# A two-layer conditioned attention kernel: reordering and rebuilding the work of its first 65 microseconds

## The chip, the cores and the metric

The kernel runs on one core of a Trainium2 chip. The metric is device time in microseconds (us), lower is better. A core has five engines with instruction queues of their own: PE (TensorE, matrix products into PSUM), ACT (ScalarE), DVE (VectorE), POOL (GpSimd) and SP (SyncE, which here issues all DMAs). They wait for each other through semaphores only.

## The reference, cut to what matters

32 batches of 256 tokens with 256 features pass through two attention layers. Layer 0 is softmax attention with 16 heads of 16 features, layer 1 is linear attention. Each ends in a modulation whose scale and shift come from an embedding `cond` of 512 numbers per batch.

```python
# layer 0, x: (32, 256, 256), emb: (32, 512)
xn = layer_norm(x) * norm_w + norm_b
q = (xn @ q_w + q_b).reshape(B, T, 16, 16);  k, v likewise
att = einsum('bnhl,bmhl->bnmh', q, k) + (1.0 - mask) * -1000000.0
y = einsum('bnmh,bmhl->bnhl', softmax(att, axis=2), v)      # over the keys
e = silu(emb) @ emb_w + emb_b                               # (32, 512) @ (512, 512)
scale, shift = split(e)
h = layer_norm(y) * sb_norm_w + sb_norm_b
x = x + silu(h * (1 + scale) + shift) @ out_w + out_b
# layer 1: q softmaxed over a head's 16 features, k softmaxed over the tokens, then
# y = q @ (k^T v) per head; the same modulation, with weights film_emb_W of its own
```

The rows that a layer norm's bias adds to a product (`norm_b @ q_w` and the like) are worked out once, at the start, and added to the projections' biases.

## The kernel before

One program keeps the work of all batches in a pipeline that is written out by hand: a turn `t` is one batch's step, with eight slots `i` in a turn, and each engine walks through `for t: for i: slot(t, i)` in that fixed order. Batch `t` enters in turn `t`:

- slot 0: PE turns the normed rows (`xturn`); slot 1: ACT copies the result rounded (`xturned`, `xT`), DVE makes its low part (`xlow`);
- slots 2, 4, 6: PE multiplies by the query, key and value weights (`qk(t, 0)`, `qk(t, 1)`, `vals`), each as three products of high and low parts; ACT adds the bias (`qk`), POOL splits the sum in a high and a low part (`split`, semaphores `s_hi`, then `s_lo`), and SP copies the parts of 16 heads into the layout of the scores (`parts`, tiles `Qs`, `Ks`; key rows 7 of 32 get the mask from DRAM, `mask_parts`);
- from 13 slots later on (`LAG_M`): PE makes scores for the row maximum (`rowmax`, eight per batch, tile `psM`) and DVE reduces them (`reduce`, tile `cm`). `psM` is there once, so each `rowmax` waits for the reduce of the one before;
- from 26 slots later on (`LAG_S`): the scores again, their exponentials (ACT) and the product with the values (`values`), four heads side by side in column tiles of the array;
- layer 1 follows in rounds of its own (`second`), after the last turn of layer 0.

What happens once stands between these slots. In turn 0 PE makes `column` (query bias, key bias) and `row` (value bias, from which DVE makes `vbx`, which the last matmul of `vals` adds). From slot (1, 5) to (2, 4) PE makes the embeddings' product, a piece `embed(c)` in each slot: 128 columns of the weights `EW` are the stationary side, and the 32 columns of `cT` (the activated embeddings, turned) stream. In (2, 1) to (2, 6) stand the bias columns and rows of layer 1. Some names in the rows: L1033 is a product of parts, L1052 `column`, L1059 `row`, L1065 `embed`, L1088 the scores, L1103 `rowmax`, L1124 `values`, L1155 `xturn`, L801 the reduce of a `rowmax`, L381 and L384 the split's high and low part, L263 and L266 the copies of `parts`.

Of the kernel before, what the change touches and what calls it, by code (L numbers as in the profile page):

```python
# [51 lines left out]
def bass_cond_seq_kernel(nc, x, cond, mask_f, mask_i, weights, emb, cols, rows, ident_d, diag_d, fill, out):  # L52
# [4 lines left out]
    with ExitStack() as ctx:  # L57
# [128 lines left out]
        p_fill, p_vb, s_cond = sem("p_fill"), sem("p_vb"), sem("s_cond")  # L186
        s_md = sem("s_md")
# [28 lines left out]
        def _(sp):  # L216
# [39 lines left out]
            def parts(n, w):  # L256

                sp.wait_ge(s_lo, 2 * n + w + 1)
                if n >= RING:
                    sp.wait_ge(s_sT, 8 * (n - RING) + 8)  # L260
                dst, b = (Qs, Ks)[w][n % RING], s_in[w][n % RING]
                for r, part in enumerate(((0, 1, 0), (0, 0, 1))[w]):
                    sp.dma_start(dst[r:128:4, :, :], qp[w][:, part, :, :]).then_inc(b, 16)  # L263
                if w:
                    for o in range(2):
                        sp.dma_start(dst[64 * o + 7:64 * o + 64:32, :, :],  # L266
                                     md[n].rearrange("c (a t) -> c a t", a=1).to_broadcast([2, 8, T])).then_inc(b, 16)
# [227 lines left out]
        def _(a):  # L495
# [164 lines left out]
            def slot(t, i):  # L660
# [53 lines left out]
        def _(v):  # L714
# [56 lines left out]
            def film(step):  # L771
                if step == 0:
                    v.wait_ge(p_act, 6)
# [190 lines left out]
            def slot(t, i):  # L964
# [8 lines left out]
                if (t, i) == (1, 4):  # L973
                    v.wait_ge(p_act, 4)
# [5 lines left out]
                if (t, i) == (2, 7):  # L980
                    v.wait_ge(p_pe, 7)
                    v.tensor_tensor(rb[:, 2, :], rb[:, 2, :], psT[1][:, 0:256], ALU.add)
                    v.tensor_tensor(rb[:, 3, :], rb[:, 3, :], psT[1][:, 512:768], ALU.add).then_inc(p_ve, 1)
# [42 lines left out]
        def _(pe):  # L1026
# [293 lines left out]
            def slot(t, i):  # L1320
                if (t, i) == (0, 1):
                    pe.wait_ge(s_ld[1], 16 * LOADS[1])
                if t == 0 and i in (1, 3):
                    pe.wait_ge(s_lw[i // 2], 16)
                    column(psM[i // 2][:, 0:2], 0, i // 2).then_inc(p_pe, 1)
                if (t, i) == (0, 3):
# [13 lines left out]
                if (t, i) == (1, 5):  # L1340
                    pe.wait_ge(p_act, 4)
                    pe.wait_ge(p_film, 2)
                    pe.wait_ge(s_ld[2], 16 * LOADS[2])
                if (t, i) == (3, 2):
                    pe.wait_ge(p_act, 6)
# [19 lines left out]
                if (t, i) == (2, 3):  # L1365
                    column(psT[0][:, 514:516], 1, 2)
                if (t, i) == (2, 5):
                    row(psT[1][:, 0:256], 1, 0)
                if (t, i) == (2, 6):
                    row(psT[1][:, 512:768], 1, 2).then_inc(p_pe, 1)  # L1370
# [83 lines left out]
```

## Time and profile before

| | us |
|---|---|
| three runs | 988.84, 990.59, 982.50 (median 988.84) |
| the profiled execution | 986.95 |
| its span, first to last instruction | 985.2 |

| engine | busy us | share of the span |
|---|---|---|
| PE | 929.1 | 94% |
| DVE | 771.3 | 78% |
| ACT | 708.9 | 72% |
| POOL | 584.9 | 59% |

Busy time is that of the recorded instructions. PE's clock has two levels, 2.4 GHz (granted clock 1.00) and half of it (0.50); the profile gives the mean of a stretch. Between 140 and 540 us it is 1.00. The chain that ended last is followed back from the last instruction, each piece with its start and its length.

### The profile page before, as it was taken

Reading aid. Unit: us, or ns where it says so; the run is one execution under the profiler, and the core shown is the slowest. Engines: PE = TensorE matmul, PEld = TensorE weight load, DVE = VectorE, ACT = ScalarE, POOL = GpSimd, SP = SyncE. Lnnn points to the kernel's source line nnn. Section 1 sums busy time; section 2 is a strip of 40 time slices with the busy share of each in tenths; the row PEclk is TensorE's granted clock in tenths of the full one; section 3 lists DMA queues with packets and bytes.
Section 4 is the critical chain, followed back from the end, with each engine's and each line's share of the span. In section 5 each row is a group of like instructions: output and inputs, shape, how many; then the busy total and the mean of one; then the engine's idle time right before and its main releaser. Section 6 shows DMA issues by size and latency. Waiting matters only on the chain.

```text
span 985.2 us, 24979 instructions
## 1 busy us (share of the span) xinstructions
PE 929.1 (94%) x8916; PEld 774.2 (79%) x8916; DVE 771.3 (78%) x1536; ACT 708.9 (72%) x1326; POOL 584.9 (59%) x1033
## 2 busy tenths in 40 slices
PE   5989999999999999999999757999999999999996
PEld 5867676777777777777777435999999999999995
DVE  5357998888888888888887734788888888888874
ACT  2137677777777777777777665688888888888874
POOL 3234364646464646464646134688888888888874
PEclk9689999999999999999999988999999999999998
DMA  6733333343434343333333222112222322223111
GB/s 223 244 100 136 114 135 136 118 153 117 154 126 146 112 158 133 138 134 137 135 126 122 93 71 71 60 65 76 77 76 89 99 79 76 77 77 92 56 28 54
DMA packets 77403, 108.63 MB, mean 110 GB/s; under 512 B 7072, under 2 KB 43392, under 8 KB 77152
## 3 DMA queue, kind: packets, MB, share of 16 engines
q1 hardware_dynamic: 77280, 107.03, 32.2%
q8 instruction: 72, 1.18, 0.5%
q14 instruction: 51, 0.42, 0.1%
HBM read 35.60 MB, written 16.88 MB: 53 GB/s over the span
## 4 chain that ended last, share of the span: by engine, by line
PE 82%; DVE 7%; issue 6%; POOL 2%; ACT 1%; DMA 1%; SPq 1%; POOLq 0%; DVEq 0%; ACTq 0%
PE psX L1033 14%; PE psY L1124 12%; PE psT L1033 10%; PE psM L1033 9%; PE psM L1103 8%; PE psT L1088 7%; PE psY L1033 4%; PE psT L1272 3%; PE psT L1044 3%; PE psM L1044 3%; PE psY L1241 3%; DVE sb_cm L801 3%; PE psY L1143 2%; DVE sb_yr L818 2%; PE psX L1044 1%
## 5 line engine op out<-in xcount | busy, mean ns | idle before, releaser
L801 DVE TENSOR_REDUCE sb_cm<-psM 128x4 f32<-128x1024 f32 x256 | 313.5, 1224 | 98.1 <-PE psM L1103 89.3
L511 ACT ACTIVATE sb_P<-psT 128x1024 f32<-128x1024 f32 x256 | 262.1, 1025 | 16.9 <-PE psT L1088 13.7
L1124 PE MATMUL psY<-sb_P,sb_Vp 128*17 128x256 f32 x2048 | 137.9, 387 | 8.8 <-DVE sb_yr L818 8.3
L367 POOL TENSOR_SCALAR sb_ve<-sb_mv 128x2 f32<-128x2 f32 x32 | 7.1, 222 | 230.3 <-DVE sb_mv L826 230.3
L1103 PE MATMUL psM<-sb_Ks,sb_Qs 64*128 64x256 f32 x1024 | 119.9, 312 | 12.2 <-DVE sb_cm L801 10.7
L1088 PEld LDWEIGHTS psT<-sb_Qs,sb_Ks 64*128 64x128 f32 x1024 | 78.2, 188 | 60.2 <-issue 54.0
L1088 PE MATMUL psT<-sb_Qs,sb_Ks 64*128 64x256 f32 x1024 | 119.8, 313 | 0.0
L525 ACT ACTIVATE sb_qp<-psX,sb_bq 128x256 f32<-128x256 f32 x122 | 51.2, 471 | 79.8 <-PE psX L1033 77.7
L1103 PEld LDWEIGHTS psM<-sb_Ks,sb_Qs 64*128 64x128 f32 x1024 | 78.4, 188 | 31.9 <-DVE sb_cm L801 14.9
L1033 PE MATMUL psX<-sb_xT,sb_W0h 128*128 128x256 f32 x488 | 96.0, 300 | 0.8
L1124 PEld LDWEIGHTS psY<-sb_P,sb_Vp 128*17 128x17 f32 x2048 | 49.4, 97 | 53.2 <-issue 15.6
L384 POOL TENSOR_TENSOR sb_qp<-sb_qp 128x512 fp32r<-128x512 f32 x64 | 82.5, 1290 | 5.3
L1033 PEld LDWEIGHTS psX<-sb_xT,sb_W0h 128*128 128x128 f32 x488 | 73.2, 196 | 6.5 <-DVE sb_xT L808 6.3
L381 POOL TENSOR_SCALAR sb_qp<-sb_qp 128x512 fp32r<-128x512 f32 x64 | 39.8, 622 | 49.5 <-ACT sb_qp L525 47.6
L549 ACT ACTIVATE sb_yT<-psY 128x256 f32<-128x256 f32 x128 | 49.3, 385 | 23.9 <-PE psY L1124 23.9
L418 POOL TENSOR_TENSOR sb_rs<-sb_ve,sb_ph 128x2 f32<-128x2 f32 x64 | 54.6, 854 | 5.3
L1033 PE MATMUL psT<-sb_W1l,sb_xT 128*128 128x256 f32 x256 | 51.6, 283 | 0.0
L1033 PE MATMUL psT<-sb_W1h,sb_xTl 128*128 128x256 f32 x256 | 51.6, 283 | 0.0
L1033 PE MATMUL psT<-sb_W1h,sb_xT 128*128 128x256 f32 x256 | 51.6, 283 | 0.0
L1033 PE MATMUL psX<-sb_xT,sb_W0l 128*128 128x256 f32 x244 | 50.4, 289 | 0.0
L534 ACT ACTIVATE sb_Vp<-psX,sb_mT 128x256 f32<-128x256 f32 x60 | 25.2, 470 | 29.7 <-PE psX L1176 29.7
L442 POOL TENSOR_SCALAR sb_v<-sb_v,sb_kd 128x256 f32<-128x256 f32 x64 | 30.5, 487 | 21.7 <-DVE sb_kd L885 21.7
(176 smaller groups left out, 2462.0 us busy)
## 6 DMA issues: line engine op xcount, KB each, us to landing
sb_Qs<-sb_qp SPq DMA_DIRECT2D x96, 256.0 KB
sb_Ks<-sb_qp SPq DMA_DIRECT2D x96, 256.0 KB
sb_xt<-in_x SPq DMA_DIRECT2D x32, 256.0 KB, 2.8
y_normed<-sb_Yn SPq DMA_DIRECT2D x32, 256.0 KB, 2.0
sb_u<-in_x SPq DMA_DIRECT2D x32, 256.0 KB, 2.9
sb_u<-y_normed SPq DMA_DIRECT2D x32, 256.0 KB, 3.1
out<-sb_w SPq DMA_DIRECT2D x32, 256.0 KB, 2.2
sb_v<-key_mask SPq DMA_DIRECT2D x32, 128.0 KB, 3.4
```

The lines of the kernel that those rows point to most:

```text
L381: g.tensor_scalar(qp[w][:, 0, :, :].bitcast(F32R), qp[w][:, 1, :, :], 1.0, 0.0, ALU.mult, ALU.add)\
L384: g.tensor_tensor(qp[w][:, 1, :, :].bitcast(F32R), qp[w][:, 1, :, :], qp[w][:, 0, :, :], ALU.subtract)\
L418: g.tensor_tensor(rs[:, k], ve[:, k], ph[:, :], ALU.pow).then_inc(e_rs[l], 1)
L511: a.activation(P[G % 4][:, :], psT[G % 2][:, :], ACT.Exp).then_inc(s_ex, 1)
L525: ins = a.activation(qp[w][:, 1, o, :], home("qk"[w], n)[:, T * o:T * o + T], ACT.Identity, bias=bq[:, 2 * w + o:2 * w + o + 1])
L549: a.activation(yT[n % 2][:, gr, :], psY[:, 0:T], ACT.Identity).then_inc(s_ye, 1)
L801: v.tensor_reduce(cm[n % 2][:, 4 * j:4 * j + 4], psMM[:, :].rearrange("p (k t) -> p k t", k=4), AX.X, ALU.max, negate=True).then_inc(s_mx, 1)
L1033: ins = pe.matmul(dst, part(lhs[a], d, o), part(rhs[b], d, r), start=(m == 0), stop=(last and m == 5))
L1044: ins = pe.transpose(dst[:, a, 128 * b:128 * b + 128], src[b][:, 128 * a:128 * a + 128], ident[:, :])
L1088: ins = pe.matmul(psT[G % 2][:, c:c + 256], Ks[n % RING][p:p + 64, g, 128 * m:128 * m + 128].bitcast(F32R), Qs[n % RING][p:p + 64, g, :].b ...
L1103: ins = pe.matmul(psM[o][:, 256 * k:256 * k + 256], Qs[n % RING][p:p + 64, j, 128 * k:128 * k + 128].bitcast(F32R), Ks[n % RING][p:p + 64, ...
L1124: ins = pe.matmul(psY[32 * j:32 * j + 17, 0:T], Vp[n % RING][:, m, 4 * gr + j, :], Pj[:, c0:c0 + 256], start=(m == 0), stop=(m == 1))
```

## The change

Five things are changed.

1. `parts`: SP sends what needs no split (masks, zeros) before it waits for the split, the high parts when POOL has made them (`s_hi`), and the low part after `s_lo`. Before, it waited for `s_lo` and then sent everything.
2. Turn 0: the keys' product comes ahead of the keys' bias `column` and the values' `row` (these move from slots 1 and 3 to slots 1 and 5), and DVE prepares the keys' weights before the statistics of batch 1.
3. The embeddings: `embed(l)` has the four 32-column pieces of `cT` as stationary sides of four column tiles, and streams 512 columns of the weights through each. The four partial sums stand in four groups of 32 partitions; ACT copies them to `es`, and `gather` adds them up and turns them with `sum4`, a stack of four 32x32 identities (made by DVE from `ident`). Layer 0's half is done in slot (1, 7), layer 1's in (2, 1), the gathers in (2, 3) and (2, 5).
4. Layer 1's value row, which nothing reads, is no longer made; its query row moves from (2, 5) to (2, 7), and DVE adds it in (3, 0).
5. The waits for the embeddings' weights (`s_ld[2]`) and layer 1's weights (`s_ld[3]`) move from (1, 5) and (2, 1) to (1, 7) and (2, 3).

```diff
@@ SP, parts(n, w) @@
-                sp.wait_ge(s_lo, 2 * n + w + 1)
                 if n >= RING:
                     sp.wait_ge(s_sT, 8 * (n - RING) + 8)
                 dst, b = (Qs, Ks)[w][n % RING], s_in[w][n % RING]
-                for r, part in enumerate(((0, 1, 0), (0, 0, 1))[w]):
-                    sp.dma_start(dst[r:128:4, :, :], qp[w][:, part, :, :]).then_inc(b, 16)
                 if w:
...
+                sp.wait_ge(s_hi, 2 * n + w + 1)
+                for r in ((0, 2), (0, 1))[w]:
+                    sp.dma_start(dst[r:128:4, :, :], qp[w][:, 0, :, :]).then_inc(b, 16)
+                sp.wait_ge(s_lo, 2 * n + w + 1)
+                sp.dma_start(dst[1 + w:128:4, :, :], qp[w][:, 1, :, :]).then_inc(b, 16)
@@ ACT, slot(t, i) @@
-                if (t, i) == (2, 5):
-                    a.wait_ge(p_pe, 6)
-                    a.activation(ev[:, :, :, :], psT[0][:, 0:8 * B].rearrange("p (l o b) -> p l o b", l=2, o=4),
-                                 ACT.Identity).then_inc(p_act, 1)
+                if (t, i) in ((1, 7), (2, 1)):
+                    l = 1 - i // 7
+                    a.wait_ge(p_pe, 6 + l)
+                    a.activation(es[:, l, :], psT[0][:, 512 * l:512 * l + 512], ACT.Identity).then_inc(p_act, 1)
...
@@ DVE, slot(t, i) @@
                 if (t, i) == (1, 4):
+                    v.tensor_reduce(sum4[:, :], ident[:, :].rearrange("p (j b) -> p b j", j=4), AX.X, ALU.add)\
+                        .then_inc(p_sum, 1)
...
                 if (t, i) == (0, 1):
+                    first_weight(1)
                     stats(1, 0)
                     stats(1, 1)
-                    first_weight(1)
@@ PE @@
-            def embed(c):
+            def embed(l):
+
                 for k in range(4):
-                    ins = pe.matmul(psT[0][:, B * c:B * c + B], EW[:, c // 4, k, 128 * (c % 4):128 * (c % 4) + 128],
-                                    cT[:, k, :], start=(k == 0), stop=(k == 3))
+                    ins = pe.matmul(psT[0][32 * k:32 * k + 32, 512 * l:512 * l + 512], cT[:, k, :], EW[:, l, k, :],
+                                    start=True, stop=True)
+                return ins
+
+            def gather(l):
+
+                for o in range(4):
+                    c = 4 * B * l + B * o
+                    ins = pe.matmul(psT[1][:, c:c + B], es[:, l, 128 * o:128 * o + 128], sum4[:, :], start=True,
+                                    stop=True)
                 return ins
@@ PE, slot(t, i) @@
-                if 13 <= 8 * t + i < 21:
-                    ins = embed(8 * t + i - 13)
-                    if (t, i) == (2, 4):
-                        ins.then_inc(p_pe, 1)
+                if (t, i) == (1, 7):
+                    pe.wait_ge(s_ld[2], 16 * LOADS[2])
+                    embed(0).then_inc(p_pe, 1)
                 if (t, i) == (2, 1):
+                    pe.wait_ge(s_v, 2)
+                    embed(1).then_inc(p_pe, 1)
+                if (t, i) == (2, 3):
                     pe.wait_ge(s_ld[3], 16 * LOADS[3])
-                    pe.wait_ge(s_v, 2)
-                    column(psT[0][:, 512:514], 1, 1)
...
```

Where the instructions stand. First SP, a batch's key and query parts, batch 1, before:

```order
L263 DMA sb_Qs<-sb_qp 32x4x512 [waits s_lo,p_fill]
L263 DMA sb_Qs<-sb_qp 32x4x512 x2
L269 DMA sb_Qs<-sb_zero 4x16x128
L263 DMA sb_Ks<-sb_qp 32x4x512 [waits s_lo]
L263 DMA sb_Ks<-sb_qp 32x4x512 x2
L266 DMA sb_Ks<-mask_parts 2x8x256 x2
```

and now:

```order
L269 DMA sb_Qs<-sb_zero 4x16x128 [waits p_fill]
L272 DMA sb_Qs<-sb_qp 32x4x512 [waits s_hi]
L272 DMA sb_Qs<-sb_qp 32x4x512
L274 DMA sb_Qs<-sb_qp 32x4x512 [waits s_lo]
L266 DMA sb_Ks<-mask_parts 2x8x256 x2
L272 DMA sb_Ks<-sb_qp 32x4x512 [waits s_hi]
L272 DMA sb_Ks<-sb_qp 32x4x512
L274 DMA sb_Ks<-sb_qp 32x4x512 [waits s_lo]
```

One copy is left behind the low part instead of three and the masks. Next PE in turn 0, from the queries' product on (W0h, W0l are the parts of the weights), now:

```order
L1041 MATMUL psT<-sb_xT,sb_W0h 128x256 [waits s_w0]
L1041 MATMUL psT<-sb_xT,sb_W0h 128x256
L1041 MATMUL psT<-sb_xT,sb_W0l 128x256 x2
L1041 MATMUL psT<-sb_xT,sb_W0h 128x256 x4
L1041 MATMUL psT<-sb_xT,sb_W0l 128x256 x2
L1041 MATMUL psT<-sb_xT,sb_W0h 128x256 x2
L1060 MATMUL psM<-sb_col,sb_W 128x1 [waits s_lw1]
L1060 MATMUL psM<-sb_col,sb_W 128x1 x3
L1067 MATMUL psY<-sb_W,sb_col 128x256 [waits s_lw2]
L1067 MATMUL psY<-sb_W,sb_col 128x256
L1041 MATMUL psT<-sb_W0l,sb_xT 128x256 [waits p_pool,s_w0]
```

The column and the row (L1060, L1067) stood ahead of these twelve matmuls of the keys; now they stand between them and the values' product. Last PE from the first row maximum of batch 0 (L1120) on, turns 1 and 2, now:

```order
L1120 MATMUL psM<-sb_Ks,sb_Qs 128x256 [waits s_mx]
L1120 MATMUL psM<-sb_Ks,sb_Qs 128x256 x3
L1074 MATMUL psT<-sb_EW,sb_cT 32x512 [waits s_ld2]
L1074 MATMUL psT<-sb_EW,sb_cT 32x512 x3
L1120 MATMUL psM<-sb_Ks,sb_Qs 128x256 [waits s_mx]
L1120 MATMUL psM<-sb_Ks,sb_Qs 128x256 x3
L1172 MATMUL psX<-sb_ident,sb_xn 128x128 [waits s_qf,s_xn]
L1172 MATMUL psX<-sb_ident,sb_xn 128x128 x3
L1120 MATMUL psM<-sb_Ks,sb_Qs 128x256 [waits s_mx]
L1120 MATMUL psM<-sb_Ks,sb_Qs 128x256 x3
L1074 MATMUL psT<-sb_EW,sb_cT 32x512 [waits s_v]
L1074 MATMUL psT<-sb_EW,sb_cT 32x512 x3
```

Before, each of the first eight row maxima was followed by a group of four such matmuls of shape 128x32 (L1065); now two of them are followed by four of shape 32x512, and two later ones by a gather.

## Rows read from the trace of the kernel before

**Rows 1.** The page: the chain that ended last, by engine.

```profile
PE 82%; DVE 7%; issue 6%; POOL 2%; ACT 1%; DMA 1%; SPq 1%; POOLq 0%; DVEq 0%; ACTq 0%
```

**Rows 2.** Chain of waits, turn 0: start us, length us, what.

```profile
14.73 1.50 PE psM L1052 x8
16.23 1.92 PE psY L1059 x4
18.15 2.57 PE psT L1033 x12
...
22.44 1.28 POOL sb_qp L384
...
25.63 0.55 SPq L266
...
26.22 3.08 DMA sb_Ks<-mask_parts
```

**Rows 3.** Windows: us; busy by engine; granted clock; DMA.

```profile
29.40:64.70 35.30, 33.25 (x194) 29.20 (x194) 16.28 (x20) 6.02 (x17) 10.62 (x18) 0.71 0.54 180
31.30:37.70 6.40, 6.40 (x31) 5.73 (x31) 1.64 (x3) 0.62 (x2) 3.21 (x6) 0.50 0.84 289
41.20:51.40 10.20, 10.20 (x50) 9.29 (x48) 3.19 (x4) 1.34 (x3) 0.00 (x0) 0.50 0.41 132
54.90:58.30 3.40, 3.40 (x17) 2.92 (x16) 0.42 (x1) 0.99 (x3) 0.70 (x3) 0.52 0.61 222
140.00:540.00 400.00, 394.53 (x4371) 289.47 (x4364) 335.50 (x520) 301.78 (x489) 215.66 (x394) 1.00 0.38 134
```

**Rows 4.** Timeline of PE: start, us, line, shapes, idle before.

```profile
29.43 0.50 PE L1103 MATMUL psM<-sb_Ks,sb_Qs 64*128 64x256 f32 x4 [1.20 <-DMA sb_Ks<-mask_parts]
53.55 1.08 PE L1065 MATMUL psT<-sb_cT,sb_EW 128*128 128x32 f32 x8
59.59 1.13 PE L1059 MATMUL psT<-sb_W,sb_col 128*128 128x256 f32 x4
64.69 0.66 PE L1155 MATMUL psX<-sb_ident,sb_xn 128*128 128x128 f32 x4
76.12 1.06 PE L1124 MATMUL psY<-sb_P,sb_Vp 128*17 128x256 f32 x16
```

**Rows 5.** Chain of waits, turns 1 to 3.

```profile
32.05 1.84 PE psT L1065 x8
...
57.88 1.24 DVE sb_cm L801
...
73.90 1.63 PE psX L1033 x12
```

**Rows 6.** Timelines of ACT and DVE, turns 0 to 2.

```profile
18.18 0.42 DVE L967 TENSOR_TENSOR sb_rb<-sb_rb,psY 128x256 f32<-128x256 f32 x1
...
18.97 0.42 DVE L971 TENSOR_TENSOR sb_vbx<-sb_rb,sb_vbx 64x256 fp32r<-64x256 f32 x1
...
20.80 0.84 ACT L525 ACTIVATE sb_qp<-psT,sb_bq 128x256 f32<-128x256 f32 x2 [4.12 <-PE psT L1033]
...
41.11 0.60 ACT L517 ACTIVATE sb_xT<-psX 128x512 fp32r<-128x512 f32 x1 [3.19 <-PE psX L1155]
...
42.88 0.68 DVE L808 TENSOR_TENSOR sb_xT<-psX,sb_xT 128x512 fp32r<-128x512 f32 x1
```

**Rows 7.** A later turn: timelines of POOL, SP and PE.

```profile
242.45 1.29 POOL L384 TENSOR_TENSOR sb_qp<-sb_qp 128x512 fp32r<-128x512 f32 x1
245.05 1.29 POOL L384 TENSOR_TENSOR sb_qp<-sb_qp 128x512 fp32r<-128x512 f32 x1
247.83 1.10 POOL L358 TENSOR_SCALAR sb_xn<-sb_xt,sb_nm,sb_rs 128x256 f32<-128x256 f32 x2
...
243.77 2.15 SPq L263 DMA_DIRECT2D sb_Qs<-sb_qp  x3
...
249.86 0.66 PE L1155 MATMUL psX<-sb_ident,sb_xn 128*128 128x128 f32 x4
```

More of the change, by code:

```diff
@@ L134, in bass_cond_seq_kernel @@
             ev = sb("ev", [128, 2, 4, B], scope=first)
+            es = sb("es", [128, 2, 2 * D], scope=first)
+            sum4 = sb("sum4", [128, B], scope=first)
             mrow, mr2, mr3, keep = (sb(f"m{i}", [B, T], scope=first) for i in range(4))
@@ L186, in bass_cond_seq_kernel @@
         p_fill, p_vb, s_cond = sem("p_fill"), sem("p_vb"), sem("s_cond")
+        p_sum = sem("p_sum")
         s_md = sem("s_md")
@@ L772, in film @@
                 if step == 0:
-                    v.wait_ge(p_act, 6)
+                    v.wait_ge(p_act, 7)
                     for l in range(2):
@@ L979, in slot @@
                     v.tensor_scalar(cT[:, :, :], cT[:, :, :], 0.5, None, ALU.mult).then_inc(p_film, 1)
[L980 to L983, printed above, removed]
+                if (t, i) == (3, 0):
+                    v.wait_ge(p_pe, 9)
+                    v.tensor_tensor(rb[:, 2, :], rb[:, 2, :], psT[0][:, 0:256], ALU.add).then_inc(p_ve, 1)
                 if t == 5 and i % 2 == 1:
@@ L1322, in slot @@
                     pe.wait_ge(s_ld[1], 16 * LOADS[1])
[L1323 to L1326, printed above, removed]
+                if (t, i) == (0, 1):
+                    pe.wait_ge(s_lw[0], 16)
+                    column(psM[0][:, 0:2], 0, 0).then_inc(p_pe, 1)
+                if (t, i) == (0, 5):
+                    pe.wait_ge(s_lw[1], 16)
+                    column(psM[1][:, 0:2], 0, 1).then_inc(p_pe, 1)
                     pe.wait_ge(s_lw[2], 16)
@@ L1342, in slot @@
                     pe.wait_ge(p_film, 2)
-                    pe.wait_ge(s_ld[2], 16 * LOADS[2])
                 if (t, i) == (3, 2):
-                    pe.wait_ge(p_act, 6)
+                    pe.wait_ge(p_act, 7)
                     pe.wait_ge(p_ve, 5)
@@ L1356, in slot @@
                     rowmax(n, j)
-                if 13 <= 8 * t + i < 21:
-                    ins = embed(8 * t + i - 13)
-                    if (t, i) == (2, 4):
-                        ins.then_inc(p_pe, 1)
+                if (t, i) == (1, 7):
+                    pe.wait_ge(s_ld[2], 16 * LOADS[2])
+                    embed(0).then_inc(p_pe, 1)
                 if (t, i) == (2, 1):
+                    pe.wait_ge(s_v, 2)
+                    embed(1).then_inc(p_pe, 1)
+                if (t, i) == (2, 3):
                     pe.wait_ge(s_ld[3], 16 * LOADS[3])
-                    pe.wait_ge(s_v, 2)
-                    column(psT[0][:, 512:514], 1, 1)
-                if (t, i) == (2, 3):
-                    column(psT[0][:, 514:516], 1, 2)
+                    pe.wait_ge(p_act, 5)
+                    pe.wait_ge(p_sum, 1)
+                    gather(0)
+                    column(psT[1][:, 512:514], 1, 1)
                 if (t, i) == (2, 5):
-                    row(psT[1][:, 0:256], 1, 0)
-                if (t, i) == (2, 6):
-                    row(psT[1][:, 512:768], 1, 2).then_inc(p_pe, 1)
+                    pe.wait_ge(p_act, 6)
+                    gather(1)
+                    column(psT[1][:, 514:516], 1, 2).then_inc(p_pe, 1)
+                if (t, i) == (2, 7):
+                    row(psT[0][:, 0:256], 1, 0).then_inc(p_pe, 1)
                 if i == 0 and ok(t):
```

10 lines of the change are left out of this document (6 added, 4 removed).

## The prediction

> **What bounds the kernel now.** I read the chain of waits first: PE carries 82% of it [rows 1]. From 140 to 540 us PE is busy 394.5 of 400 us at a clock of 1.00 [rows 3]. Nothing in that stretch is changed but the order of SP's copies, so what the front gives up or wins passes straight to the end. The question is then how early a fixed point of the front comes. I take PE's `xturn` of batch 3, at 64.69 [rows 4]: behind it the instructions of PE are the same in both kernels.
>
> Ahead of it two stretches differ. Up to the first `rowmax` at 29.43 the chain runs through `column`, `row`, the keys' product, ACT, POOL's split, SP's copies and the mask's landing, and PE idles 1.20 us for it [rows 2, 4]. From there to 64.69 are 35.3 us in which PE is busy 33.3, but at a mean clock of 0.71: 6.4 us, 10.2 us and 3.4 us of it at half clock, 20 us in all [rows 3]. In the first two PE is busy all the time by its records. The reader is to see two things in these rows: PE bounds this stretch, and busy is not fast. A piece of `embed` takes 1.84 us there [rows 5] and 1.08 at the full clock [rows 4], for eight matmuls that stream 32 columns each.
>
> **Part 1, up to the first `rowmax`.** PE's keys' product no longer stands behind 1.50 us of `column` and 1.5 of `row` (16.23, to the next product at about 17.6) [rows 2]. It can start at about 14.5 instead of 17.6. But ACT adds the keys' bias, which needs `column`, and that now runs after the product: 14.5 + 2.6 + 1.5 = 18.6, then some 0.6 for the bias. ACT starts on the keys at about 19.2, not at 20.80 [rows 6]. POOL's high part follows 0.9 later, the low part ends 1.3 after that, at about 22.2; one copy stands behind it, not three and two of the mask. The last key copy is issued at about 22.2, where the mask was at 26.2, and lands 3.1 later by that row [rows 2]: 25.3, with 3 us to spare. The wait of 1.20 is gone; what is late next is PE itself, which ends batch 1's keys at 28.2.
>
> PE has the same work before that, in another order, with one price. `row` now stands directly ahead of the values' product, whose last matmul waits for DVE to make `vbx` of it: from 18.18 to 19.39 in the trace, 1.2 us [rows 6]. Six matmuls cover 0.7 to 1.3 of it. I take 0.4 us as lost; the bounds are 0 (cover holds) and 1.5 (DVE's three steps twice as long beside POOL's split, which now falls there). First `rowmax`: 28.2 + 0.4 + 0.1 = 28.7, a gain of 0.7 (bounds -0.3 and +1.2). DVE's new `sum4` is a reduce of 128 columns in a stretch in which DVE waits for ACT; I cost it at nothing, and at 0.3 if that cover is gone.
>
> **Part 2, from there to `xturn` 3 at the full clock.** I write it slot by slot with durations from full-clock rows. A `rowmax` occupies PE for 0.45, its reduce takes 1.24 [rows 5] with 0.1 of handing over, so two `rowmax` are at least 1.8 apart. A key or query product is 1.65 (1.63 in [rows 5]), the values' product, 14 matmuls for 12, 1.8. `embed(l)` is 8 passes of 512 columns in four column tiles; `values` is 16 passes of 256 in four such tiles, the same streaming, and takes 1.0 (76.12 to the next instruction) [rows 4]. `gather(l)` has the shape of an old piece, 1.0 [rows 4], a `column` 0.9, the `row` 0.95 (1.13 with its drain) [rows 4].
>
> `rowmax` 0 at 28.7, 1 at 30.5; values' product to 32.7; 2 at 32.7; `embed(0)` ends at 34.2 under the reduce; 3 at 34.5; `xturn` 2 to 35.6; 4 at 36.3; `embed(1)` to 37.8 under the reduce. Here the change adds a wait: ACT copies `es` for layer 1 (0.6) before it copies `xT` (0.60), and DVE's `xlow` (0.68) [rows 6] and the queries' product of batch 2 stand behind: 37.8 + 0.1 + 0.6 + 0.6 + 0.7 = 39.85. PE idles about 1.2 us, since `rowmax` 5 ends at 38.6. Queries to 41.5; 6 at 41.5; gather and column to 43.9; 7 to 44.4; keys to 46.05; 8; gather and column to 48.4; 9; values' product to 50.7; 10, row, to 52.1; 11; `xturn` 3 at 52.55. Against 64.69 that is 12.1 us, part 1 included.
>
> The other edits: the dropped `row` is in this sum. ACT's copies of `es` and the rest lie beside PE except where named. The weights for which PE waits in (2, 3) were issued at about 28 and landed within 7 us; SP now sends them some 4 us earlier, and PE needs them at 42. No other wait of SP is reached later than before.
>
> **Part 3, the clock.** The sum holds at 1.00; the trace had 0.71. What PE did before its clock fell: at 31.3, 1.20 us of idle and a piece of `embed`; at 41.2 and 54.9, pieces, a `column`, a `rowmax`. Before it rose, at 37.7, 51.4 and 58.3, it had done a whole product of 256-column matmuls. The change takes away most of the small things: 64 matmuls of 32 columns become 16 of 512 and 16 of 32. But from 38.15 to 48.4 my schedule has five `rowmax` and two products, 5.5 us of 10.2 that stream 256 columns, and nothing in the rows shows such a mixture. Bounds: no half clock, nothing lost; the old share of 20 in 35.3 us, where each such us costs up to half, T = 23.85 + 0.28 T = 33.3, so 9.4 lost at most. I take something between, nearer the lower end because of what goes: 5.5 us of half clock, 2.7 us lost. **Gain 12.1 - 2.7 = 9.4 us.**
>
> The Trainium skill (TensorE: Matmul & The Clock Gate, the section on HAM oscillation) speaks against the change here: it says that gaps between bursts of matmuls throttle the clock, and that the remedy is to keep PE busy. By it the old stretches, without a gap, should have kept the clock, which the trace denies, 0.50 at a busy share of 100% [rows 3]; and the new schedule, with gaps, should be the colder one. That is the second rival below, at its cold end.
>
> **Part 4, the turns after.** In a later turn the copies are issued as soon as POOL's split is done (243.77 behind the subtract that ends at 243.74 [rows 7]), and `LAG_M` has them wanted half a turn and more later. Sending parts earlier only adds slack. I cost it at nothing; what it costs if it slows POOL is the last rival.
>
> Sum against the profiled execution: 986.95 - 9.4 = 977.55. That execution lies 1.9 under the median of three runs that spread over 8; for a median I add half of it: **978.5 us**.
>
> **Rivals.**
> - *The clock never falls in the front.* For it: the streaming replaces the small matmuls in every place. Against: the 1.2 us of idle behind `xT`. Gain 12.1, time 975.8. Chance 0.22.
> - *The clock stays as cold as it was.* For it: in the walk four of the twelve `rowmax` wait for a reduce, with less than before to fill the gap. Against: 20 us of half clock hung on work that is gone. The share kept, T is at most 33.3 and rather 31, since the half clock costs nothing where PE waits anyway; gain 3 to 6.5, say 4.5, time 983.4. Chance 0.32.
> - *The four column tiles run one after the other*, so the change doesn't do what it says. Then `embed(l)` costs four times a `row` of two 256-column matmuls, 4 x 0.95 = 3.8 instead of 1.0, and `es` delays `xT` by as much: 2 x 2.8 lost, gain 12.1 - 5.6 - 2.7 = 3.8, time 984. Against: `values` in the same tiling needs 1.0 us for 16 passes of 0.2 each [rows 4]. Chance 0.04.
> - *Slower.* Since the high parts now leave while POOL still subtracts for the low part of the same tile, POOL's subtract (1.29) could be slowed by the copies, in every one of 32 turns. POOL's chain of a turn, split, `csplit`, split, normalization, ends at 248.93 and PE's `xturn` that needs it is at 249.86 [rows 7]: 0.9 us of slack for two subtracts. From 0.5 us more per subtract on it decides; to eat the front's gain and 1% besides, 19 us in 32 turns, it needs 0.6 a turn over the slack, 0.75 per subtract, so 2.0 us instead of 1.29; time 999. Against: at 245.05 a subtract ran while the copies of the query parts, issued from 243.77, were under way, and took 1.29 as the one at 242.45 without them [rows 7]. Chance 0.02.
>
> **How the numbers follow.** The forecast's own case has 0.40: half clock for 2 to 8 us, 976.8 to 981. About 1% is what a measurement of this kernel can tell from no change, 9.9 us, so the border to faster lies at 979.0. Faster takes the first rival and a bit over half of the forecast's case and little of the second: 0.22 + 0.23 + 0.02 = 0.47. Slower 0.02. The rest, 0.51, is within 1%. The range reaches from a full gain with a fast execution, 973.5, to the cold and the serial case with a slow one, 985.5; beyond are about 0.1 on each side.
>
> **What would show it.** Right: the first `rowmax` at 28.3 to 29.2 with no wait for a DMA; `embed` groups of eight matmuls in about 1.0 us (1.9 at half clock) between 33 and 38; PE waiting 1 to 1.5 us for `xlow` at about 39; `xturn` 3 at 52 to 58; a granted clock above 0.8 between the first `rowmax` and it; the same length from there to the end, about 920.5 us. Wrong: a wait of the values' product for `vbx` of over 1 us; `xturn` 3 beyond 60 at a clock of about 0.7; or a later part that is not 920.5, which would mean that the front isn't passed on, or that its half-clock stretches between 560 and 620 us came out otherwise, which no part of this sum covers.

## The result, and the profile after

The changed kernel takes 976.94 us, the median of four runs (973.07 to 978.56), against 988.07 us of four runs before (982.5 to 990.59). The ratio is 0.9896, with a 95% interval of 0.9854 to 0.9938. The forecast was 978.5. The profiled executions stand at 977.76 and 986.95, so 9.2 us lie between the two traces, where the sum had 9.4.

The chain of the changed kernel by engine, which answers to [rows 1]:

```profile
PE 82%; DVE 8%; issue 6%; POOL 2%; ACT 1%; SPq 0%; DMA 0%; POOLq 0%; DVEq 0%; ACTq 0%
```

DMA and SP's queue have fallen from 1% to under half a per cent of it, and DVE has gained one. Windows of the changed kernel, columns as in [rows 3]: the front stretch, a piece of it, and all that is left behind `xturn` 3.

```profile
29.95:55.50 25.55, 21.48 (x159) 16.47 (x158) 15.94 (x19) 6.90 (x19) 11.61 (x19) 0.93 0.55 184
45.50:48.60 3.10, 3.10 (x16) 2.88 (x16) 1.22 (x1) 0.19 (x1) 0.74 (x3) 0.52 0.70 259
55.50:976.00 920.50, 877.33 (x8627) 728.22 (x8625) 740.77 (x1478) 694.86 (x1290) 561.22 (x990) 0.98 0.31 104
```

From the first `rowmax` to `xturn` 3 there were 35.3 us at a clock of 0.71 and are now 25.55 at 0.93. What is left at half clock is 3.1 us at 45.5. The last row is 920.5 us long, and so it was before (985.2 - 64.69): in these two executions all of the gain lies ahead of the fixed point. The higher clock isn't a matter of one execution either: over the whole span its mean was 0.980 to 0.989 in the four runs of the changed kernel, and 0.970 to 0.977 in the 14 of the kernel before that stand beside group 3 below.

PE's timeline of the changed kernel, for [rows 4] and the slots of the forecast's walk:

```profile
15.21 0.64 PE L1041 MATMUL psT<-sb_xT,sb_W0h 128*128 128x256 f32 x4
...
16.17 0.95 PE L1060 MATMUL psM<-sb_col,sb_W 128*128 128x1 f32 x8
16.98 1.11 PE L1067 MATMUL psY<-sb_W,sb_col 128*128 128x256 f32 x4
20.87 0.50 PE L1041 MATMUL psT<-sb_W0l,sb_xT 128*128 128x256 f32 x2 [2.78 <-DVE sb_W0l L758]
...
22.79 1.05 PE L1041 MATMUL psT<-sb_W0h,sb_xT 128*128 128x256 f32 x4
...
29.95 0.50 PE L1120 MATMUL psM<-sb_Ks,sb_Qs 64*128 64x256 f32 x4
...
34.50 1.06 PE L1074 MATMUL psT<-sb_EW,sb_cT 128*32 128x512 f32 x8
...
41.14 0.51 PE L1041 MATMUL psX<-sb_xT,sb_W0h 128*128 128x256 f32 x2 [1.10 <-DVE sb_xT L815]
...
43.20 1.08 PE L1082 MATMUL psT<-sb_sum,sb_es 128*128 128x32 f32 x8
...
46.46 1.05 PE L1041 MATMUL psX<-sb_xT,sb_W0h 128*128 128x256 f32 x4
...
55.50 0.66 PE L1172 MATMUL psX<-sb_ident,sb_xn 128*128 128x128 f32 x4
```

The reader is to see four things. The first `rowmax` waits for no DMA, but it isn't earlier: it stands at 29.95, where it was at 29.43 [rows 4]. In its place there is a wait of 2.78 us ahead of the values' product, for DVE's `W0l`, which the forecast doesn't have. `embed` takes 1.06 us for eight passes of 512 columns, so the four column tiles run side by side. And a group of four 256-column matmuls takes 0.64 us at 15.21 and 1.05 at 22.79 and 46.46: that pair of numbers tells the clock from the rows themselves.

DVE and POOL of the changed kernel beside each other (timelines, columns as in [rows 6] and [rows 7]):

```profile
15.77 2.17 DVE L1012 TENSOR_SCALAR sb_xn<-sb_xt,sb_mv,sb_rs 128x256 f32<-128x256 f32 x2 [1.49 <-POOL sb_nm L356]
17.86 0.60 DVE L753 TENSOR_SCALAR sb_W0h<-sb_W,sb_col 128x256 fp32r<-128x256 f32 x2
18.50 2.31 DVE L758 SCALAR_TENSOR_TENSOR sb_W0l<-sb_W,sb_col,sb_W0h 128x256 fp32r<-128x256 f32 x2
20.74 0.41 DVE L974 TENSOR_TENSOR sb_rb<-sb_rb,psY 128x256 f32<-128x256 f32 x1
...
21.51 0.42 DVE L978 TENSOR_TENSOR sb_vbx<-sb_rb,sb_vbx 64x256 fp32r<-64x256 f32 x1
```

```profile
15.82 0.62 POOL L386 TENSOR_SCALAR sb_qp<-sb_qp 128x512 fp32r<-128x512 f32 x1
16.53 1.27 POOL L389 TENSOR_TENSOR sb_qp<-sb_qp 128x512 fp32r<-128x512 f32 x1
18.53 0.62 POOL L386 TENSOR_SCALAR sb_qp<-sb_qp 128x512 fp32r<-128x512 f32 x1 [0.73 <-ACT sb_qp L530]
19.23 1.30 POOL L389 TENSOR_TENSOR sb_qp<-sb_qp 128x512 fp32r<-128x512 f32 x1
```

Two things moved here. DVE's `xn` of batch 1 used to follow POOL's statistics at 14.69 and to take 0.73 for its two steps; since DVE now makes the keys' weights ahead of `stats`, it begins at 15.77, beside POOL's split of the queries, and takes 2.17. (Two steps merged in a row: `x2`.) And the split of the keys, whose subtract stood at 22.44 [rows 2] and now at 19.23, falls beside `W0l`: 2.31 for two steps that take 0.88 without POOL (at 12.31 in the same trace). POOL loses nothing by it here. The kernel before had one such place already, which [rows 6] leaves out, its `W0l` of the values beside the split of the queries:

```profile
15.98 2.12 DVE L751 SCALAR_TENSOR_TENSOR sb_W0l<-sb_W,sb_col,sb_W0h 128x256 fp32r<-128x256 f32 x2
```

The Trainium skill (SBUF — State Buffer, Terms) says that DVE and GpSimd arbitrate for one pair of ports, that the pair is held for a whole instruction, and that the loser blocks. The rows agree: the steps at 17.86, while POOL is idle, take their usual 0.60, and so does the add at 20.74 with 0.41. In the execution of e7 (below) POOL comes second: its first step begins at 19.21, under `W0l`, and takes 0.86 for 0.62. Here DVE is the one that is held, even at 18.50, where by the records its step begins 0.03 us ahead of POOL's and takes 0.91 of those 2.31; POOL's subtracts take 1.27 and 1.30, beside 1.29 in [rows 7].

### The profile page after: what moved, and what is told of

The parts are those of the page before. It is cut to its first block, busy times and chain, and to the rows that moved or that the text cites. A ratio compares the mean times of both kernels' runs of the same rounds, so it can differ in the third digit from the quotient of the medians.

```text
span 976.0 us, 24849 instructions
## 1 busy us (share of the span) xinstructions
PE 916.1 (94%) x8880; PEld 760.1 (78%) x8880; DVE 772.6 (79%) x1536; ACT 709.6 (73%) x1328; POOL 581.9 (60%) x1033
## 4 chain that ended last, share of the span: by engine, by line
PE 82%; DVE 8%; issue 6%; POOL 2%; ACT 1%; SPq 0%; DMA 0%; POOLq 0%; DVEq 0%; ACTq 0%
PE psX L1041 14%; PE psY L1141 13%; PE psM L1041 10%; PE psT L1041 9%; PE psM L1120 8%; PE psT L1105 7%; PE psY L1041 4%; PE psT L1289 3%; PE psT L1052 3%; PE psM L1052 3%; PE psY L1258 3%; DVE sb_cm L808 3%; PE psY L1160 2%; DVE sb_yr L825 2%; PE psX L1052 1%
## 5 line engine op out<-in xcount | busy, mean ns | idle before, releaser
L1120 PE MATMUL psM<-sb_Ks,sb_Qs 64*128 64x256 f32 x1024 | 118.5, 309 | 11.8 <-DVE sb_cm L808 11.6
L1120 PEld LDWEIGHTS psM<-sb_Ks,sb_Qs 64*128 64x128 f32 x1024 | 77.5, 186 | 32.9 <-DVE sb_cm L808 17.3
L389 POOL TENSOR_TENSOR sb_qp<-sb_qp 128x512 fp32r<-128x512 f32 x64 | 82.4, 1287 | 5.4
L847 DVE TENSOR_TENSOR sb_v<-psM,sb_u 128x512 f32<-128x512 f32 x32 | 22.1, 692 | 26.8 <-PE psM L1041 26.8
```

Of the source, the lines that this page charges most:

```text
L389: g.tensor_tensor(qp[w][:, 1, :, :].bitcast(F32R), qp[w][:, 1, :, :], qp[w][:, 0, :, :], ALU.subtract)\
L1120: ins = pe.matmul(psM[o][:, 256 * k:256 * k + 256], Qs[n % RING][p:p + 64, j, 128 * k:128 * k + 128].bitcast(F32R), Ks[n % RING][p:p + 64, ...
```

## The experiments

A time is a median with its range; the ratio, with a 95% interval, is to runs of the kernel before on the same chip, whose medians were 987.46 (26 runs), 987.63 (9) and 987.06 (14) in the three groups. It is the record's own figure and not the quotient of the medians: the two can differ by 0.0025, so differences of medians between kernels are good to 2 or 3 us. Edits are abridged. With each stands the trace's first `rowmax` (F), `xturn` 3 (X), and the granted clock between them.

### Group 1: one part at a time

**e1: DVE's `stats` ahead of the keys' weights again.**

```
-    first_weight(1)
     stats(1, 0)
     stats(1, 1)
+    first_weight(1)
```

> The changed kernel with one piece undone: in slot (0, 1) DVE makes the statistics of batch 1 before the keys' weights again. Theory (DVE's new order costs the front): POOL's normalization comes 1.2 us earlier and out of the way of its first split, DVE's xn and the values' weights no longer run beside two splits (2.17 and 2.31 us, against 0.73 and 2.12), the values' product of batch 0 no longer waits 2.8 us, xturn 1 starts at 20 to 21 us instead of 23.86, the first rowmax at 26.2 to 27.2 instead of 29.95, xturn 3 at about 52, time about 974.5. Rival (it is PE's new order, the row directly ahead of the values' product, that makes the wait): xturn 1 stays beyond 22.5, the first rowmax beyond 28.7, time 976 to 978.

Measured: 978.24 us (976.32 to 979.76, 7 runs), ratio 0.9931 (0.99 to 0.9961); F 30.50, X 56.01, clock 0.93. I had expected 974.5; time and first `rowmax` are those of the rival. The wait moved, it didn't go. PE, DVE and POOL of this execution:

```profile
21.42 0.38 PE L1193 MATMUL psT<-sb_vbx,sb_c 128*128 128x256 f32 x1 [2.03 <-DVE sb_vbx L978]
```

```profile
14.91 0.73 DVE L1012 TENSOR_SCALAR sb_xn<-sb_xt,sb_mv,sb_rs 128x256 f32<-128x256 f32 x2 [0.49 <-POOL sb_nm L356]
...
19.18 0.70 DVE L976 CAST sb_vbx<-sb_rb 128x256 fp32r<-128x256 f32 x1
19.92 1.45 DVE L978 TENSOR_TENSOR sb_vbx<-sb_rb,sb_vbx 64x256 fp32r<-64x256 f32 x1
```

```profile
19.12 0.62 POOL L386 TENSOR_SCALAR sb_qp<-sb_qp 128x512 fp32r<-128x512 f32 x1 [1.08 <-ACT sb_qp L530]
19.82 1.26 POOL L389 TENSOR_TENSOR sb_qp<-sb_qp 128x512 fp32r<-128x512 f32 x1
```

`xn` is back at 0.73, so DVE's order did that. But now `vbx` lies beside the keys' split: its cast takes 0.70 (0.29 alone), its subtract 1.45 (0.42 alone), and each ends 0.1 to 0.3 after the step of POOL that it lay beside. Each of the two theories has half of it: the order delays `xn`, and `row` behind the keys' product puts `vbx` where POOL works.

**e2: the embeddings alone.** SP's copies, PE's `column` and `row` and DVE's order of the kernel before, with the new `embed`, `gather` and the dropped row.

```
-    if (t, i) == (0, 1): ... column(0)
-    if (t, i) == (0, 5): ... column(1); row
+    if t == 0 and i in (1, 3): ... column(i // 2)
+    if (t, i) == (0, 3): ... row
```

> The kernel before with parts 3 to 5 of the change alone: embeddings as column tiles, gather, row dropped; SP's copies, PE's column and row and DVE's order in turn 0 as before. Theory (the gain is the embeddings' alone): first rowmax at 29.4 behind the mask's landing, then about 25.5 us to xturn 3, at 55, time 977 to 978, the same as the whole change. Rival (sending parts early and the keys' product carry a good part of it): xturn 3 beyond 58, time 980 or more.

Measured: 977.65 us (974.55 to 980.18, 8 runs), ratio 0.9914 (0.9885 to 0.9944); F 29.29 with 1.21 us of waiting for the mask, X 57.11, clock 0.82. By the medians this part alone saves 9.8 us, where the whole change saves 11.1 (by the ratios 8.5 and 10.3). The intervals of the two ratios overlap, so what the other parts add can't be told from nothing.

**e3: SP's copies alone,** in the kernel before.

```
-                sp.wait_ge(s_lo, 2 * n + w + 1)
...
+                sp.wait_ge(s_hi, 2 * n + w + 1)
...
+                sp.wait_ge(s_lo, 2 * n + w + 1)
```

> The kernel before with SP's new order of copies alone. Theory: the copies land before PE is done with batch 1's keys, so only the wait of 1.20 us goes; first rowmax at 28.3, nothing in the later turns (from xturn 3 to the end 920.5 us), about 1 us less. Rival (the slower rival of the prediction: copies of high parts slow POOL's subtract): the subtract takes over 1.4 us in the mean and the later part grows.

Measured: 984.02 us (981.12 to 988.46, 8 runs), ratio 0.9981 (0.9952 to 1.0011); F 28.61, X 65.94, clock 0.68. The wait of 1.20 us is gone, as PE shows,

```profile
28.61 0.50 PE L1105 MATMUL psM<-sb_Ks,sb_Qs 64*128 64x256 f32 x4
```

and the stretch behind it is 37.33 us long, 2.0 more than before, at a colder clock (this execution, 988.46, was the slowest of the eight). Nothing reaches the end that can be told from no change: the interval contains 1. From X to the end are 920.8 us, and POOL's subtract has a mean of 1290 ns in this trace, as in the kernel before. The page of the changed kernel:

```profile
L389 POOL TENSOR_TENSOR sb_qp<-sb_qp 128x512 fp32r<-128x512 f32 x64 | 82.4, 1287 | 5.4
```

So the early copies don't slow the subtract in the 32 turns: the slower rival is false.

**e4: the embedding in one tile,** accumulated over 32 output rows instead of spread over four column tiles; the copy to `es` and the gather use these 32 rows.

```
-    pe.matmul(psT[0][32 * k:32 * k + 32, ...], cT[:, k, :], EW[:, l, k, :], start=True, stop=True)
+    pe.matmul(psT[0][0:B, ...], cT[:, k, :], EW[:, l, k, :], start=(k == 0), stop=(k == 3))
```

> The changed kernel with the four pieces of an embedding's product in one column tile, added up in PSUM, the gather over 32 rows: the same streams without the concurrency. Theory (four tiles run at the same time): embed takes 3.5 to 3.8 us at the full clock instead of 1.04, some 2.3 us more for each beyond the reduce that covers it, partly given back by a steadier clock; xturn 3 at 58 to 60.5, time 980 to 983. Rival (the passes would overlap in one tile too, or the cover is larger): embed below 2 us, time within 1 us of the change.

Measured: 979.55 us (977.49 to 982.56, 10 runs), ratio 0.9937 (0.9905 to 0.9969); F 28.45, X 58.78, clock 0.94.

```profile
32.99 3.62 PE L1074 MATMUL psT<-sb_EW,sb_cT 128*32 128x512 f32 x8
```

3.62 against 1.06: the tiles do overlap, 3.4 times. The price is less than expected (980 to 983). Twice 2.56 us more lengthen F to X by 4.8, at about the same clock; the median is 2.6 above the changed kernel's, some 4 by the ratios.

### Group 2: the wait in front, and what sets the clock

**e5: `row` ahead of the keys' product,** the keys' `column` behind it, DVE's order as in e1.

```
-    if (t, i) == (0, 5): ... column(psM[1], 0, 1); row(psY, 0, 2)
+    if (t, i) == (0, 3): ... row(psY, 0, 2)
+    if (t, i) == (0, 5): ... column(psM[1], 0, 1)
```

> The changed kernel with DVE's statistics ahead of the keys' weights again, and the values' row ahead of the keys' product (the keys' column stays behind it). Theory (DVE's small-matrix steps are slow only beside POOL's splits, and what delays the values' product is whichever of them falls there): vbx is made from about 16 to 18 us, partly beside the queries' split, well ahead of the values' product, which runs without a wait; xturn 1 at 19.5 to 21 instead of 23.86, the first rowmax at 26 to 27.5, xturn 3 at about 52 to 53 plus what half clock takes, time 974 to 975. Rival (DVE's values' weights, not vbx, are late in this order too): the values' product waits over 1 us for sb_W0l, xturn 1 at 22 or later, time as the change.

Measured: 972.97 us (971.44 to 973.15, 4 runs), ratio 0.9838 (0.9817 to 0.9859): below both kernels by the median, and its interval touches that of the changed one only at the edge (0.9854). F 26.45, X 50.54, clock 1.00.

```profile
18.04 0.41 DVE L974 TENSOR_TENSOR sb_rb<-sb_rb,psY 128x256 f32<-128x256 f32 x1
18.48 0.29 DVE L976 CAST sb_vbx<-sb_rb 128x256 fp32r<-128x256 f32 x1
18.81 0.42 DVE L978 TENSOR_TENSOR sb_vbx<-sb_rb,sb_vbx 64x256 fp32r<-64x256 f32 x1
```

```profile
16.49 1.34 POOL L389 TENSOR_TENSOR sb_qp<-sb_qp 128x512 fp32r<-128x512 f32 x1
20.34 0.62 POOL L386 TENSOR_SCALAR sb_qp<-sb_qp 128x512 fp32r<-128x512 f32 x1 [2.50 <-ACT sb_qp L530]
```

```profile
26.45:50.54 24.09, 20.01 (x158) 15.19 (x158) 15.95 (x19) 6.89 (x19) 11.62 (x19) 1.00 0.75 244
```

`vbx` is made in the 2.5 us in which POOL is idle, at its plain 0.29 and 0.42, PE doesn't wait for it, and `xturn` 1 comes at 20.55, not at 23.86. So the wait came of DVE's steps falling beside POOL's split. And F to X, without any half clock, is 24.09 us: the walk of the forecast had 23.85.

**e6: e5, with the second copy of `es` one slot later,** behind `xT`.

```
-    if (t, i) in ((1, 7), (2, 1)):
+    if (t, i) in ((1, 7), (2, 2)):
```

> The kernel of e5 with ACT's copy of es for layer 1 one slot later, behind xT of batch 2. Theory: the queries' product of batch 2 no longer waits 1.10 us for xlow, gather(1) in (2, 5) is still late enough; xturn 3 some 1.1 us earlier than in e5 at an equal clock, time 973 to 974. Rival (the reduce chain of the row maxima bounds here, not xT): xturn 3 moves by under 0.3 us at an equal clock.

Measured: 972.47 us (970.26 to 974.95, 4 runs), ratio 0.9837 (0.981 to 0.9864); F 26.75, X 50.99, clock 0.93. PE in this execution:

```profile
36.34 0.50 PE L1120 MATMUL psM<-sb_Ks,sb_Qs 64*128 64x256 f32 x4 [0.33 <-DVE sb_cm L808]
36.94 0.51 PE L1041 MATMUL psX<-sb_xT,sb_W0h 128*128 128x256 f32 x2
```

The wait of 1.10 us for `xlow` is gone, so `es` did cause it. The time can't be told from e5: the profiled execution had half clock in the stretch (0.93), which took back what the wait had cost.

**e7 and e8: extra work of two kinds.** Both add dead matmuls to the changed kernel, once in each of eight slots: e7 four passes of 32 columns, as before the change, e8 eight passes of 256 columns. Their output isn't read.

```
+    if 13 <= 8 * t + i < 21:
e7+      4 x pe.matmul(psT[1][:, 256:256 + B], EW[...], cT[:, k, :], ...)
e8+      8 x pe.matmul(psT[1][:, 256:512], c64, vbx, ...)
```

> The changed kernel with the old pieces back as dead work: in each of the eight slots from (1, 5) on, four matmuls of 128x32 on 128-column weights (eight passes, 0.92 us at the full clock), whose result nobody reads. Theory (small matmuls let the clock fall): the stretch from the first rowmax to xturn 3 has 10 us or more at half clock, as before the change, and grows by 8 to 10 us; time 985 or more. Rival (the clock does not care, only PE time counts): it grows by what is not under a reduce, 3 to 5 us, with a clock of 0.9 or more; time 980 to 982.

> The changed kernel with other dead work in the same eight slots: eight passes of 256 fp32r columns each (about 0.95 us at the full clock), the same PE time as in e7 but dense streams. Theory: the clock stays at 1.00 from the first rowmax to xturn 3, which grows by 3 to 5 us; time 979 to 982, less than e7. Rival (the clock falls at the same places whatever streams): as e7, 985 or more.

Measured: e7 983.38 us (979.38 to 984.62, 6 runs), ratio 0.9943 (0.9922 to 0.9964); e8 980.1 us (979.71 to 980.76, 4 runs), ratio 0.9916 (0.9892 to 0.994). Windows from F to X, e7 and then e8:

```profile
28.72:60.15 31.43, 30.36 (x223) 25.31 (x222) 15.95 (x19) 6.89 (x19) 11.60 (x19) 0.89 0.48 163
```

```profile
28.57:58.83 30.26, 29.73 (x223) 24.33 (x222) 16.02 (x19) 6.90 (x19) 11.68 (x19) 0.94 0.55 186
```

In the small form a group takes 1.08 us, in the wide one 1.22, and still the wide kernel is 3.3 us faster in the median; five of e7's six times lie above all four of e8's, the sixth below them. That is the direction expected, but it isn't firm: the intervals of the ratios overlap, and of the 2.7 us between the two spans 1.4 lie behind X, where the instructions are the same. And the size was missed: I expected e7 at 985 or more with at least 10 us at half clock, and 0.89 of 31.43 is 6.9 us (2 x 0.11 x 31.43). A clock of 0.89 is also within what executions of this stretch without any added work had, 0.82 (e2) to 1.00 (e5), and over the whole span e7's six runs had 0.982 to 0.988, no less than the changed kernel's 0.980 to 0.989. So e7 doesn't show that small matmuls bring the cold clock back.

### Group 3: the other direction, and SP's copies again

**e9: the kernel before, with four dead passes of 256 columns ahead of each piece of `embed`.**

```
     if 13 <= 8 * t + i < 21:
+        4 x pe.matmul(psT[1][:, 256:512], c64, vbx, ...)
         ins = embed(8 * t + i - 13)
```

> The kernel before, with dead work ahead of each of its eight pieces of embed: four passes of 256 fp32r columns (0.48 us at the full clock), 32 matmuls more in all and nothing taken away. Theory (the old stretch was cold because PE streamed little of its busy time): from the first rowmax to xturn 3 the clock rises from 0.71 to 0.9 or more, the stretch gets no longer than the 35.3 us of before in spite of up to 3.8 us of added work, time 984 to 988. Rival (the clock has nothing to do with the streams): the clock stays at 0.68 to 0.75 and the stretch grows to 39 us or more, time 991 or more.

Measured: 985.11 us (981.22 to 988.04, 10 runs), ratio 0.9982 (0.9961 to 1.0002); F 28.89, X 62.78.

```profile
28.89:62.78 33.89, 32.57 (x225) 28.79 (x225) 16.28 (x20) 5.99 (x17) 10.62 (x18) 0.85 0.57 187
```

The kernel before, given 32 more matmuls, gets through this stretch in 1.4 us less (33.89 for 35.26), as its clock goes from 0.71 to 0.85. I expected 0.9 or more. These are single executions, but the runs bear it out: over the whole span the ten of e9 had a mean clock of 0.977 to 0.982, the 14 of the kernel before beside them 0.970 to 0.977, and the added work made the kernel no slower (ratio at most 1.0002). Nothing was removed here, so the half clock isn't a matter of PE having too much to do.

**e10: the changed kernel with SP's copies of before; e11: e5 with them.**

```
-    sp.wait_ge(s_hi, ...); two high copies; sp.wait_ge(s_lo, ...); one low copy
+    sp.wait_ge(s_lo, ...); three copies; then masks or zeros
```

> The changed kernel with SP's old order of copies. Theory (PE is late in the changed kernel, so the copies have slack): the last key part is issued at about 23.5 us and lands at about 26.6, ahead of the first rowmax at 29.95 or, in an execution like that of e7, 28.6; no wait for a DMA, time 976 to 978, the same as the change. Rival (the new order of copies carries part of the gain, in the later turns too): a wait of over 0.5 us at the first rowmax or a later part above 921, time 979 or more.

> The kernel of e5 with SP's old order of copies. Theory: PE is ready for the first rowmax at 26.4; the keys' low part is ready at 22.3, three copies and two masks behind it are issued by 25.3 and the last lands at 27.9 to 28.4; the first rowmax waits 1.5 to 2 us for it, xturn 3 comes 1 to 2 us later than in e5, time 974 to 975. Rival (the copies land in time anyway): first rowmax within 0.3 us of e5's 26.45, time as e5.

Measured: e10 978.27 us (973.97 to 979.69, 5 runs), ratio 0.9915 (0.9885 to 0.9945); F 28.61, X 52.70, clock 1.00. e11 976.85 us (975.77 to 977.54, 4 runs), ratio 0.9897 (0.9867 to 0.9928), with

```profile
28.60 0.50 PE L1118 MATMUL psM<-sb_Ks,sb_Qs 64*128 64x256 f32 x4 [1.37 <-DMA sb_Ks<-mask_parts]
```

Both are slower than I expected, e10 by 0.3 us and e11 by 1.9. In the change as it is, the early copies are worth nothing that can be measured: PE itself is late, and no DMA is waited for. Once PE comes 2 us earlier (e5), the mask is the last again. Without the early copies the median is 976.85 and not 972.97, and the two ratio intervals don't touch. Of these 3.9 us the trace shows 1.37 as the wait itself. It has PE ready at 27.23 where e5 had it at 26.45, and F to X takes 26.62 us at a clock of 0.87 (X is 55.22) where e5 had 24.09 at 1.00. The four runs of e11 are the colder ones too, 0.981 to 0.984 over the whole span against 0.985 to 0.987. Whether the wait brought that on isn't shown.

## Why the prediction was right

**Part 1, the first `rowmax` at 28.7: right in four executions, by 1.25 us wrong in the one profiled, and not for the reason given.** The instructions up to there are those of the change in e4, e7, e8 and e10 (but for SP's copies in e10), and their first `rowmax` stand at 28.45, 28.72, 28.57 and 28.61. The step that failed is "PE has the same work before that, in another order, with one price". The price was mis-sized, and the order itself won time, which the forecast didn't have.

First, the price was 1.9 us and not 0.4. PE in e4, where the waits are 0.77 and 1.13:

```profile
19.38 0.50 PE L1041 MATMUL psT<-sb_W0l,sb_xT 128*128 128x256 f32 x2 [0.77 <-DVE sb_W0l L758]
...
21.49 0.38 PE L1193 MATMUL psT<-sb_vbx,sb_c 128*128 128x256 f32 x1 [1.13 <-DVE sb_vbx L978]
```

I had bounded the wait for `vbx` at 1.5 with DVE's steps "twice as long beside POOL's split"; its subtract was over three times as long (1.41 in e4, 1.45 in e1, for 0.42). The trace of before already had more than twice, the 2.12 for 0.88 above. And DVE's own moved lines, `first_weight` ahead of `stats`, the forecast didn't cost at all. Its own sign of being wrong, a wait for `vbx` of over 1 us, came up in all four of these executions (1.13 to 1.15), and in e1 (2.03).

Second, PE reaches its full speed sooner. In the kernel before, groups of four 256-column matmuls at 12.83 and at 18.80 both take 1.05 us:

```profile
18.80 1.05 PE L1033 MATMUL psT<-sb_xT,sb_W0h 128*128 128x256 f32 x4
...
20.81 0.64 PE L1033 MATMUL psT<-sb_W0h,sb_xT 128*128 128x256 f32 x4
```

The changed kernel has 0.64 from 15.21 on, and 0.95 for the `column` that took 1.70 by PE's timeline. The keys' product, done at once, comes ahead of `column` and `row`; I had walked through them with durations that were the slow ones, and called the work the same. In the six executions with this order PE is at full speed by about 15 to 16.5 us, in the four with the old one (before, e2, e3, e9) at about 19.5 to 21; why, no run tests. In e4 `xturn` 1 stands at 22.54, with 1.90 of waiting, where before it stood at 22.25 without: the order won 1.6 us. By luck the two omissions nearly cancel.

The profiled execution adds a third. There PE is about 0.5 us earlier at `column` than e4 (16.17 for 16.70), the keys' split therefore begins at 18.53 and not at 19.05, and so it falls on `W0l` (2.31) which in e4 is nearly done by then (0.88). PE waits 2.78 us in one piece, and soon after its clock falls: 0.76 in the mean from 22.0 to 28.5, where e4 has 1.00. A start that was earlier led to an end that was later.

**Part 2, the walk at full clock: right.** 24.09 us in e5 and e10 against 23.85. The walk has a slip that covers the difference: it sets `rowmax` 11 at 52.1, 1.4 after `rowmax` 10, against its own rule of 1.8, which would have added 0.4; the trace has 1.82 (53.24 to 55.06). (The sum for the end of `xlow` is 39.8, not 39.85.) `embed` 1.06 and `gather` 1.08 for 1.0 each; the wait for `xlow` 1.10 for 1.2, at 41.1, and its cause shown by e6.

**Part 3, the clock: the right case, a smaller size.** I took 5.5 us of half clock and 2.7 lost; there were 3.1 us, and the stretch is 25.55 - 24.09 = 1.5 us longer than without. So `xturn` 3 at 55.50 was forecast at 52.55 + 2.7 = 55.25: 1.25 too early by part 1, 1.24 too late by the clock, and 0.24 too early by the walk. That the sum came out within 0.25 is luck: two misses of 1.2 us cancel. The median, 976.94, lies between the forecast's 978.5 and the first rival's 975.8. In other executions of the same instructions the half clock is nought (e5, e10) or more (e2 had 0.82). Which it will be, neither the prediction nor the runs can say.

**That the clock is the source of the gain** the granted clocks show. How much of the gain it is can be estimated from the windows. At 0.71 the old stretch lost up to 0.29 x 35.26 = 10.2 us, which leaves 25.0 at full clock. In the new stretch about three quarters of what the clock took reached the length (e2: 0.18 x 27.82 = 5.0, and 3.7 longer than e5); by that share the old one lost 7.7, which leaves 27.6. The new one takes 24.09. So of the 9.7 us by which the stretch got shorter 6.2 to 8.7 are the clock's, and 0.9 to 3.5 are work that is gone or better placed. e9 points the same way: it warms the old kernel by adding to it. And e2 shows that rebuilding the embeddings does it. *What in the embeddings kept the clock down isn't shown.* e7 brought back eight groups of small matmuls and got 0.89, not 0.71, and e8 beside it is too close to decide. In e7 the two 512-column `embed` lie between those groups and the second `row` of layer 1 is gone; whether one of these keeps the clock up wasn't tried.

The Trainium skill's rule that the prediction set against the change (TensorE: Matmul & The Clock Gate, on HAM oscillation), that gaps throttle and a busy PE doesn't, is half borne out. The clock fell after the 2.78 us of idle in the changed kernel, and in e1 after 2.03 us and another 1.65 (0.53 from 22.5 to 29.0); in e4 it stood through 1.13 and 1.70. But it doesn't describe the kernel before: there the clock stood at 0.50 with PE busy in all of 10.2 us [rows 3], and more matmuls made it faster.

**Part 4: right, and to the last digit by luck.** It is 920.5 us in both, but from X to the end the eleven other executions had 918.4 (e2) to 920.8 (e3) with the same instructions of PE, 1.9 us less in e1 than in the changed kernel. So the part that the sum took as fixed moves by up to 2.4 us from one execution to the next. The half-clock stretches that the sum didn't cover lie there: from 540 to 600 and from 600 to 640 us the changed kernel has a clock of 0.89 and 0.96, e1 of 0.91 and 1.00, an estimated 2.8 us lost at most by that difference (0.02 x 60 + 0.04 x 40), beside those 1.9.

**The rivals.** *The clock never falls* was true for single executions (F to X at 1.00 in e5 and e10) and not for the one profiled; the changed kernel's fastest run, 973.07 with a mean clock of 0.989, looks like e10's (973.97, 0.989). *It stays as cold* is false (0.93). *The tiles run in a row* is false (1.06), and e4, which is that rival built, came to 979.55 where it had 984. Between the sum and the profiled execution lie 3.2 us: F to X was 1.8 shorter than the 32.15 of the sum (3.62 for 3.8 in each `embed`, 0.3 of cover, and the clock), the part behind X 1.2, the first `rowmax` 0.25 earlier. *Slower* is false: the subtract took 1287 ns, where that rival needed 2.0 us.

## What to carry to other kernels

A busy PE isn't a fast PE: compare one group of equal matmuls (here 0.64 against 1.05) along the trace before counting work, and where small moving operands fill a stretch, swapping the operands so that the stream is wide, with the column tiles, is worth a try: here it brought 8 to 10 us. When a step is moved on PE, walk through the vector engine's steps behind it too and look at what GpSimd does beside them; a DVE step can cost two to three times as much there. An early arrival is worth only what the next engine in line leaves of it: SP's copies brought nothing that could be measured until `row` had been moved, and then they saved a wait of 1.37 us. And an execution is one draw of the clock: before a difference of 2 us between two traces is explained, look at the clock of all runs.

## What the runs showed of the hardware

- DVE beside POOL's 128x512 steps: two `tensor_scalar` of 128x256 took 2.17 us for 0.73, two `scalar_tensor_tensor` 2.31 for 0.88, a cast 0.70 for 0.29, a 64x256 subtract 1.45 for 0.42. POOL's subtract kept its 1.26 to 1.34 us.
- Four column tiles of 32 with 512-column streams took 1.06 us for eight passes, one tile 3.62.
- At the start of both kernels PE's matmuls have the length of the half clock (1.05 for four of 256 columns) while the record of the granted clock says 1.00 for that window (8 to 16 us). Early in a trace the durations decide, and not that column.
- A kernel got faster in a stretch by 32 added matmuls: 35.26 to 33.89 us in one execution each; over ten runs the mean clock was 0.977 to 0.982, for 0.970 to 0.977 in 14 without them (e9).
- The same PE instructions from F to X took 24.09 us at a clock of 1.00 (e5, e10), 25.55 at 0.93, 26.62 at 0.87 (e11) and 27.82 at 0.82 (e2).
